# Moving a pair of transposes: both turns of the next half behind the projection in a relational graph layer

## The reference

```
masks = (relation[None] == rel_ids[:, None, None, None]).astype(x.dtype)
h = jnp.einsum('rbnm,bmd->rbnd', masks, x)
y = jnp.einsum('rbnd,rdo->bno', h, weight)
out = _layernorm(x + y + bias, axis=-1)
```

## Time and profile before

| | before |
|---|---|
| median of 3 runs | 154.64 us (154.24 to 154.83) |
| profiled execution, its own time | 155.23 us |
| its span, first to last instruction | 152.6 us |
| TensorE busy | 123.6 us (81%) |
| TensorE weight loads busy | 73.8 us (48%) |
| VectorE busy | 85.2 us (56%) |
| ScalarE busy | 83.2 us (55%) |
| GpSimd busy | 68.3 us (45%) |
| mean granted TensorE clock | 0.984 |

### The profile page before, as it was taken

The page is one execution under the profiler, slowest core; times in us unless marked ns, Lnnn a source line. Parts: engine busy times, 40 slices in busy tenths (PEclk is TensorE's granted clock), DMA queues, the critical chain, the costliest instruction groups (busy, mean ns, idle before and its releaser), DMA issues.

```text
span 152.6 us, 2160 instructions
## 1 busy us (share of the span) xinstructions
PE 123.6 (81%) x690; PEld 73.8 (48%) x690; DVE 85.2 (56%) x265; ACT 83.2 (55%) x83; POOL 68.3 (45%) x80
## 2 busy tenths in 40 slices
PE   0079759989898989898998989898989899898800
PEld 0056637455463636363745546363636373567600
DVE  1170363838565656657393846565655739385851
ACT  3553754482828385665748282838466674812311
POOL 1005393070857159342937095715844393203341
PEclk9999999999999999999999999999999999999985
DMA  5969999999999999999897949499921000301221
GB/s 152 427 249 424 426 409 429 419 416 420 427 418 411 419 416 431 415 419 415 296 353 282 350 129 357 137 309 313 415 85 77 0 0 4 137 0 41 99 103 41
DMA packets 7500, 42.22 MB, mean 277 GB/s; under 512 B 832, under 2 KB 1344, under 8 KB 3392
## 3 DMA queue, kind: packets, MB, share of 16 engines
q1 hardware_dynamic: 7488, 42.08, 70.3%
HBM read 37.88 MB, written 4.19 MB: 276 GB/s over the span
## 4 chain that ended last, share of the span: by engine, by line
ACT 33%; issue 27%; PE 27%; DVE 6%; DMA 3%; POOL 1%; DVEq 0%; POOLq 0%; ACTq 0%
ACT mask L164 32%; PE h_ps L183 17%; PE tp_ps L171 9%; DMA adj_sb<-in_adj_dram 3%; DVE maskT L175 2%; PE y_ps L190 1%; DVE stats L196 1%; DVE total L421 1%; POOL scale L208 1%; DVE mean_var L201 1%; ACT h_sb L352 1%; DVE above L462 0%; DVE out_sb L212 0%; DVE seen L412 0%; DVE var_eps L205 0%
## 5 line engine op out<-in xcount | busy, mean ns | idle before, releaser
L164 ACT ACTIVATE mask<-adj_sb 128x2048 fp8e4<-128x2048 int32 x32 | 61.0, 1905 | 10.2 <-DMA adj_sb<-in_adj_dram 10.2
L208 POOL TENSOR_TENSOR scale<-var_eps,power 128x4 f32<-128x4 f32 (+1 forms) x17 | 16.6, 976 | 63.3 <-issue 31.9
L175 DVE COPY maskT<-tp_ps 128x512 uint32<-128x512 uint32 x32 | 22.0, 686 | 31.4 <-PE tp_ps L171 31.4
L171 PE MATMUL tp_ps<-identity,mask 128*128 128x128 f32 x128 | 22.1, 297 | 17.2 <-ACT mask L164 17.2
L183 PE MATMUL h_ps<-maskT,x_sb 128*128 128x512 fp8e4 (+1 forms) x144 | 32.6, 369 | 3.2 <-DVE maskT L175 3.2
L183 PE MATMUL h_ps<-maskT,x_rest 128*128 128x512 fp8e4 (+1 forms) x144 | 32.6, 370 | 0.0
L183 PE MATMUL h_ps<-maskT,x_fine 128*128 128x512 fp8e4 (+1 forms) x144 | 32.6, 369 | 0.0
L352 ACT COPY h_sb<-h_ps 128x512 f32<-128x512 f32 x14 | 8.2, 587 | 39.9 <-issue 35.7
L171 PEld LDWEIGHTS tp_ps<-identity,mask 128*128 128x128 f32 x128 | 18.0, 206 | 24.0 <-ACT mask L164 16.1
L160 POOL TENSOR_TENSOR x_bias<-x_sb,bias_sb 128x1024 f32<-128x1024 f32 x8 | 19.0, 2372 | 9.9 <-DVE x_fine L157 9.9
L183 PEld LDWEIGHTS h_ps<-maskT,x_sb 128*128 128x128 bf16 x144 | 13.9, 98 | 19.1 <-DVE maskT L175 2.2
(11 more groups left out here) (22 smaller groups left out, 24.1 us busy)
## 6 DMA issues: line engine op xcount, KB each, us to landing
adj_sb<-in_adj_dram SPq DMA_DIRECT2D x32, 1024.0 KB, 12.7
x_sb<-in_x_dram SPq DMA_DIRECT2D x8, 512.0 KB, 14.5
out_dram<-out_sb SPq DMA_DIRECT2D x7, 512.0 KB, 7.0
out_dram<-out_sb SPq DMA_DIRECT2D x1, 256.0 KB, 2.0
out_dram<-out_sb SPq DMA_DIRECT2D x2, 128.0 KB, 1.9
bias_sb<-in_L_gnn_bias_dram SPq DMA_DIRECT2D x1, 64.0 KB, 9.0
w_sb<-in_L_gnn_weight_dram SPq DMA_DIRECT2D x1, 64.0 KB, 10.7
```

What stands on the lines that cost most here:

```text
L164: nc.scalar.activation(mask[:, slot % NMASK], adj_sb[:, slot % NADJ], ACT.Copy, saturate=False).then_inc(done, 1)
L171: last = nc.tensor.transpose(tp_ps[:, bank, place:place + P], words[:, o, j], identity[:, :])
L175: nc.vector.tensor_copy(maskT[:, place].rearrange("k j o p e -> k (j o p e)").bitcast(u32), tp_ps[:, bank].bitcast(u32)).then_inc(done, 1)
L208: nc.gpsimd.tensor_tensor(scale[:, slot, tiles], var_eps[:, slot, tiles], power[:, tiles], ALU.pow).then_inc(done, by)
```

## The change

In `products_half`, for halves 1 to 14, the first of the two turns leaves its place between part 0 and part 1 and goes behind the projection, directly ahead of the second turn. No instruction is added or removed, and no wait condition is changed.

```diff
@@ -562,10 +562,9 @@
                     if hf % 2 == 0:
                         x_ready(part, b)
                     last = part_products(part, b % NX, b % 2, slice(place, place + 2), hf % NBANK)
-                    if part == 0:
-                        turn(2 * hf + 2)
                     if part == 1:
                         project_half(hf - 1)
+                        turn(2 * hf + 2)
                         turn(2 * hf + 3)
                 last.then_inc(multiplied, 2)
```

## The result

The changed kernel takes 156.28 us (median; 155.87 to 156.96) against 154.52 (154.24 to 154.83): ratio 1.0118, 95% interval 1.0076 to 1.0159. It is 1.76 us slower; forecast was 156.2. In the three later rounds of measurement the kernel before had medians of 154.90, 154.48 and 155.33 us, so a median moves by up to 0.85 us from round to round; the changed kernel was measured in the first round only. One of those later executions, 259.02 us, was in a far slower state and counts in no ratio.

A forecast was written before the change was run, and what follows sets the result against it. The prediction took a TensorE-ScalarE loop of 8.25 us per half as the bound; after the change, seven pairs of 16.58 us start half 15 1.60 us later, so 154.64 + 1.60 = 156.2 us, range 154.8 to 157.4.

The forecast's parts named there:

- What bounds the kernel before: TensorE and ScalarE's first conversion form a loop of 8.25 us per half; the loop through the shift has 0.16 us slack.
- The first wait goes: TensorE's first turn moves to 4.49 us after the half's first product (T), its unit ready at T + 2.69: no wait.
- The second turn waits instead: Loop over first bank, add, statistics, shift, `finish_half`, second conversion: two halves take 16.58 us, 0.04 us longer per half.
- The emptying gets short of time: TensorE waits for VectorE to empty the second bank at half 2's start, 0.55 us late; 1.09 us lost once.
- The 0.84: Time in us by which the next half's products follow VectorE's start on the second bank.
- What no row priced: Costs of two turns in a row with the second waited for: (a), (b), and that the 0.84 might be less.
- The sum: Half 15 starts at 137.53 against 135.93, and the end moves by the same: plus 1.60 us, 156.2 us.
- the faster one: Rival: the wait is gone for good, halves bound by the second bank at 7.79 us; 149.2 us, 8 in 100.
- The two others: Rivals: no difference, 155.4 us, 15 in 100; clearly slower, (a) at its upper end, 157.1 us, 12 in 100.
- (a): First bank's delay behind its turn: 0.66 us taken, other end 0.79, which would add 0.9 us in all.
- (b): Second turn to part 2 on TensorE: 0.59 us taken, other end 0.47, which would take off 0.8 us in all.
- No difference: Rival: only the 1.09 us start loss stays, half won back by (b), 16.46 per pair; 155.4 us, 15 in 100.

The follow-up runs named there:

- the edit on ScalarE: The kernel before, with ScalarE converting both units ahead of `finish_half`: 154.79 us, 0.9996 of the kernel before.
- the copy on VectorE: The kernel before, with one more copy of the first bank on VectorE into a buffer that nothing reads: 154.78 us, 0.9999 of the kernel before.
- the kernels that cut it (148.2, 148.4): Changed kernel with both conversions ahead of `finish_half`: 148.24 us; changed kernel with `finish_half` in place but for one half earlier: 148.42 us.
- shorten it (153.9): The changed kernel, with VectorE's add ahead of the emptying of the first bank: 153.90 us, 0.9891 of the kernel before.
- lengthen it (160.4): The changed kernel, with one more copy of the first bank on VectorE, between its emptying and its folding: 160.39 us, 1.0363 of the kernel before.

## Why the prediction was right

**What bounds the kernel before** held: the edit on ScalarE and the copy on VectorE both left it at its time and at 8.25 per half.

**The first wait goes** held: the turn at T + 4.49, as forecast, without a wait.

**The second turn waits instead** held, term by term. Forecast and measured: first bank T + 5.15 and 5.17 (100.42), add T + 6.35 and 6.37, second bank T + 6.95 and 6.98 (102.23), variance T + 9.53 and 9.57 (104.82), second turn of the next half T + 14.18 and 14.19 (109.44), two halves 16.58 and 16.58 (37.52 to 136.97, six pairs). That this loop was the one to decide is shown by the kernels that cut it (148.2, 148.4), shorten it (153.9) and lengthen it (160.4), each within 0.5 us of its forecast.

**The emptying gets short of time** held, and as forecast at half 2 alone: TensorE waited 0.29 for the bank there, once. The 0.84 that I took from the start's row is 0.74 in the changed kernel (27.90 to 28.64), and half 2 began 7.73 after half 1 where 7.79 was forecast. It made no difference, as odd halves hang on odd ones: 16.61 from half 1 to 3, for 16.58. The loss named for this, 1.09, measured 1.11.

**What no row priced**: the first bank comes 0.68 behind its turn (99.74 to 100.42), near the 0.66 taken and not 0.79; and the turn that was waited for takes 0.59 until part 2 (101.44 to 102.03), not 0.47. Both costs for which the range had its bounds stayed at the value taken.

**The sum**: 1.60 forecast, 1.60 between half 1 and half 15, 1.76 between the medians. The 0.16 between the last two is within the spread of the runs. That the median came within 0.1 of 156.2 is luck, since the median of the kernel before moved by 0.85 from round to round; the 1.60 inside the traces is the firmer test.

**The rivals**: the faster one, 149.2 us, came true as soon as the finish no longer waited, at 148.2 to 148.4, with 7.73 for the 7.79 that it was given; so its mechanism exists, and what stood against it was the wait for the shift alone. The two others did not come: (a) and (b) stayed at the values taken. The text of *No difference* speaks of half of the 1.09 won back, but its sum takes 0.84 off the whole 1.60, which leaves the 0.76 that it uses.

The rule of the Trainium skill (Perfetto Trace Analysis, Optimization Strategy) is to find what a gap on the most-contended engine waits for, and to get that sooner. Taken for the first gap alone, as in the prediction's *Faster*, it gave the wrong sign here. Taken again for the gap that opened next, the second turn's, it points at the conversion behind `finish_half` (148.2 us). Taken a third time, for the wait for the second bank, it points at VectorE's order (142.9 us).

## What to carry to other kernels

Before a wait is taken away, add up the other loops that run through the same engines, over as many rounds as they span; here one lay 0.16 us behind the wait that showed, and a gain of 13 us on paper became a loss of 1.8. A step that moves later drags along what is queued behind its result: VectorE's add lost an idle 1.47 us of cover, though VectorE was busy only 56% of the time. When a loop runs over several engines, look for the in-order instruction that only happens to stand in front, here `finish_half` before a conversion and the bank before the add, and exchange it. Both exchanges together on the changed kernel gave 142.94 us, 8% under the kernel before. The first alone gave nothing on the kernel before, because there another loop was the longer.

## What the runs showed of the hardware that I had not expected

The start is the least repeatable part. In the profiled executions of the eleven kernels, which all share it, half 1 began between 20.39 and 21.92 us, a width of 1.5 us; the runs of the changed kernel lie within 1.1. In the two profiles of before and after, the products of half 0's first quarter follow each other slowly, and those of its second do not. From the timeline of the changed kernel, eight products of 256 columns each:

```profile
9.46 1.89 PE L183 MATMUL h_ps<-maskT,x_sb 128*128 128x256 fp8e4 x8 [0.79 <-DVE maskT L175]
...
11.15 1.91 PE L183 MATMUL h_ps<-maskT,x_rest 128*128 128x256 fp8e4 x8
...
12.85 1.36 PE L183 MATMUL h_ps<-maskT,x_fine 128*128 128x256 fp8e4 x8
...
14.06 0.63 PE L171 MATMUL tp_ps<-identity,mask 128*128 128x128 f32 x4
...
15.47 1.08 PE L183 MATMUL h_ps<-maskT,x_sb 128*128 128x256 fp8e4 x8 [0.79 <-DVE maskT L175]
16.39 1.07 PE L183 MATMUL h_ps<-maskT,x_rest 128*128 128x256 fp8e4 x8
```

From one group to the next the first take 1.69 us and the later ones 0.92, while the view by windows gives a granted clock of 1.00 (2.4 GHz) for 8 to 12 us and for 16 to 20 us alike; that figure does not account for the difference. The moment at which they became quick differed: the third group of the first quarter and the turn behind it began 1.21 us apart here (12.85 to 14.06), and 1.65 in the profile of before (12.96 to 14.61). That is 0.44 of the 0.56 us by which half 1 began sooner; 0.10 was there at the first product (9.56 and 9.46). I did not test what sets this point.
